# Routing stage of a fused attention and mixture-of-experts kernel: the two experts searched in the logits, softmax, token products and last remainders moved to GpSimd, other filler counts on TensorE

## What is computed

```
x = x + tanh(g_xattn[0]) * xattn(layernorm(x), ctx, itok, Wq, Wkv, Wo)
h_in = layernorm(x)
gate_logits = einsum('bsh,eh->bse', h_in, gate_w)          # E = 8
gate_probs = softmax(gate_logits, axis=-1)
top_v, top_i = top_k(gate_probs, 2)
comb_w = einsum('bsk,bske->bse', top_v, one_hot(top_i, E))
for e in range(E):
    h = silu(h_in @ w1[e] + b1[e])
    y = h @ w2[e] + b2[e]
    out = out + y * comb_w[..., e:e + 1]
x = x + tanh(g_ffn[0]) * out
```

## Time and profile before

| | |
|---|---|
| median of 3 runs | 357.06 us (356.36 to 357.26) |
| the profiled execution | 356.92 us, of which 355.1 us is the span from first to last instruction |
| TensorE, busy share of the span | 91% |
| VectorE | 76% |
| GpSimd | 58% |
| ScalarE | 49% |
| mean granted clock of TensorE | 0.978 of full |

### The profile page before, as it was taken

One profiled execution on the slowest core, in us unless ns is written; L12 is line 12 of the kernel. 1 busy time (PEld: TensorE's weight loads), 2 busy tenths in 40 slices (PEclk: granted clock), 3 DMA queues, 4 the chain that ended last, 5 costly groups with the idle time before them and its releaser, 6 DMA issues.

```text
span 355.1 us, 11441 instructions
## 1 busy us (share of the span) xinstructions
PE 322.9 (91%) x3486; PEld 266.3 (75%) x3486; DVE 269.9 (76%) x638; ACT 174.1 (49%) x490; POOL 205.9 (58%) x223
## 2 busy tenths in 40 slices
PE   8789989999977989999999999999999999999930
PEld 7457778888877877888888888888888887778710
DVE  5649999999978887778877788777887875656520
ACT  2452255565455456656555565654656543253400
POOL 3476889996752071566656757477473764662330
PEclk9999999999999899999999999999999999999985
DMA  7799999998999421232323323232332323241210
GB/s 250 246 362 412 405 420 404 404 351 327 344 384 391 119 64 34 32 60 37 56 38 64 46 47 48 50 61 38 57 48 48 53 42 61 35 68 26 33 18 13
DMA packets 31406, 53.23 MB, mean 150 GB/s; under 512 B 4834, under 2 KB 25554, under 8 KB 29300
## 3 DMA queue, kind: packets, MB, share of 16 engines
q0 software_dynamic: 9408, 26.63, 29.5%
q1 hardware_dynamic: 15972, 22.44, 17.6%
q10 hardware_dynamic: 5968, 3.39, 3.1%
HBM read 42.29 MB, written 10.17 MB: 148 GB/s over the span
## 4 chain that ended last, share of the span: by engine, by line
PE 63%; DVE 20%; issue 5%; DMA 5%; ACT 2%; POOL 2%; DVEq 0%; ACTq 0%; POOLq 0%
PE ps L1090 28%; PE ps L1104 16%; PE ps L1107 8%; DVE ps L1270 5%; DVE sel L1266 2%; PE ps L1118 2%; PE ps L1112 2%; DMA sel<-near_rows,win_near 2%; DVE w_parts L1266 2%; DMA tokens_split<-xsplit 2%; DVE xs L1302 1%; PE ps L1111 1%; PE ps L1106 1%; DMA near_rows<-w_parts 1%; DVE ps L1274 1%
## 5 line engine op out<-in xcount | busy, mean ns | idle before, releaser
L1090 PE MATMUL ps<-sel,w_parts 128*128 128x128 f16 x1776 | 141.3, 219 | 1.0 <-issue 1.0
L1090 PEld LDWEIGHTS ps<-sel,w_parts 128*128 x1776 | 119.3, 98 | 26.0 <-issue 1.8
L823 ACT ACTIVATE sel<-ps,b1T 128x128 f32<-128x128 f32 x296 | 84.3, 368 | 91.4 <-PE ps L1090 89.4
L596 POOL DMA_INDIRECT out<-sel x37 | 63.1, 1706 | 85.9 <-DVE sel L1540 74.0
L1104 PE MATMUL ps<-w_parts,sel 128*128 x259 | 96.3, 379 | 0.4
L1107 PE MATMUL ps<-w_parts,sel 128*128 x259 | 70.6, 273 | 0.0
L588 POOL DMA_INDIRECT sel<-tokens_split,sel x37 | 43.7, 1180 | 18.9 <-DVE sel L1463 12.6
L1495 DVE SCALAR_TENSOR_TENSOR sel<-sel 128x512 f16<-128x512 f32 x74 | 51.3, 694 | 2.5
L1481 DVE SCALAR_TENSOR_TENSOR w_parts<-w_parts (+1 forms) x32 | 39.0, 1220 | 8.4 <-issue 7.2
L1493 DVE TENSOR_SCALAR sel<-sel 128x512 f16<-128x512 f32 x74 | 33.2, 448 | 10.4 <-ACT sel L823 10.0
L583 POOL TENSOR_TENSOR sel<-sel 128x1 f32<-128x1 f32 x37 | 39.8, 1076 | 1.9 <-PE ps L1118 1.9
(11 more groups left out here) (221 smaller groups left out, 462.1 us busy)
## 6 DMA issues: line engine op xcount, KB each, us to landing
w_parts<-in_L_ffn_w SPq DMA_DIRECT2D x16, 1024.0 KB
out<-xs SPq DMA_DIRECT2D x16, 128.0 KB
tokens_split<-xsplit ACTq DMA_DIRECT2D x16, 128.0 KB, 6.2
xs<-in_x ACTq DMA_DIRECT2D x2, 512.0 KB, 7.1
xs<-in_x SPq DMA_DIRECT2D x2, 512.0 KB, 7.7
near_rows<-w_parts SPq DMA_DIRECT2D x4, 256.0 KB, 9.2
sel<-tokens_split,sel POOLq DMA_INDIRECT x37
out<-sel POOLq DMA_INDIRECT x37
```

Source lines behind the costliest of these rows:

```text
L596: pool.indirect_dma_start(out_rows, bass.IndirectOffsetOnAxis(slot_row[:, at(q - 1)], 0), y_sb[(k + 3) % 4], None, compute_op=ALU.add).the ...
L823: act.activation(h32[n][:, c * P:c * P + P], ps_h[n][:, c * P:c * P + P], ACT.Silu, bias=biases[:, c:c + 1], scale=1.0 / (X_SCALE * W_SCALE))\
L1090: mm = pe.matmul(ps_h[n][:, c * P:c * P + P], w, xx, start=(i == 0), stop=(i == len(products) - 1))
```

## The change

1. VectorE searches the two largest in the logits, not in the probabilities (`top_two`, then `chosen`), for tiles 0 to 10 and then 11 to 15. The subtraction of the largest logit is one GpSimd instruction over all 16 tiles, after the last of these searches; one Exp on ScalarE follows it. Sum and reciprocal stand on VectorE behind the scan, and three GpSimd products make `r_comb`.
2. The last two remainders stand on GpSimd behind these products.
3. The two products of `col_tok` with the token numbers go from VectorE to GpSimd; TensorE's first and third `rows_into_list` wait for them as well.
4. The fillers of the drain are 10, 10, 12 and 8 (before 4, 4, 8 and 4), and those ahead of `RT_CUM` 36 (before 48).

```diff
@@ GpSimd
             norms(T - 1, 1)
+            pool.wait_ge(s["rt"], RT_TOP)
+            pool.tensor_tensor(r_tmp[:, :, :], logit[:, :, :], r_m8[:, :, 0:1].to_broadcast([P, T, E]), ALU.subtract)\
+                .then_inc(s["shifts_ok"], 1)
+            pool.wait_ge(s["rt_exp"], 1)
+            pool.wait_ge(s["rt"], RT_CUM)
+            pool.tensor_scalar(r_p[:, :, :], r_ex[:, :, :], gate2[:, 0:1], None, ALU.mult).then_inc(s["comb_ok"], 1)
+            pool.wait_ge(s["comb_ok"], 1)
+            pool.tensor_tensor(r_p[:, :, :], r_p[:, :, :], r_m16[:, :, :], ALU.mult).then_inc(s["comb_ok"], 1)
+            pool.wait_ge(s["rt"], RT_INVERSE)
+            pool.wait_ge(s["comb_ok"], 2)
+            pool.tensor_tensor(r_comb[:, :, :], r_p[:, :, :],
+                               r_rs[:, :].rearrange("p (t o) -> p t o", o=1).to_broadcast([P, T, E]), ALU.mult)\
+                .then_inc(s["comb_ok"], 2)
             remainder(T - 2)
             remainder(T - 1)
-
+            for h in range(2):
+                tokens = slice(T // 2 * h, T // 2 * h + T // 2)
+                pool.wait_ge(s["rt"], RT_HOT + 1 + h)
+                pool.tensor_tensor(col_tok[:, tokens, :, :], col_tok[:, tokens, :, :], spread_pairs(tok16[:, :], NT),
+                                   ALU.mult).then_inc(s["tok_ok"], 1)
             pool.wait_ge(s["o_ps"], T)
             pool.memset(b2_wide, 0.0).then_inc(s["b2_zeroed"], 1)
@@ ScalarE
             token_out(T - 4)
-            act.wait_ge(s["rt"], RT_SHIFT)
-            act.activation(r_ex[:, 0:LATE, :], r_tmp[:, 0:LATE, :], ACT.Exp).then_inc(s["rt_exp"], 1)
             logits_kept(T - 4)
...
-            act.wait_ge(s["rt"], RT_SHIFT_LATE)
-            act.activation(r_ex[:, LATE:T, :], r_tmp[:, LATE:T, :], ACT.Exp).then_inc(s["rt_exp"], 1)
+            act.wait_ge(s["shifts_ok"], 1)
+            act.activation(r_ex[:, :, :], r_tmp[:, :, :], ACT.Exp).then_inc(s["rt_exp"], 1)
...
-            act.wait_ge(s["rt"], RT_COMB)
+            act.wait_ge(s["comb_ok"], 4)
             act.dma_start(xd.rearrange("(t p) d -> p t d", p=P)[:, :, D:XD], r_comb[:, :, :]).then_inc(s["comb_in"], 16)
@@ TensorE
             second_turn(T - 3)
-            spin(4)
+            spin(10)
             logits(T - 3)
             second_turn(T - 2)
-            spin(4)
+            spin(10)
             logits(T - 2)
+            spin(12)
+            second_turn(T - 1)
             spin(8)
-            second_turn(T - 1)
-            spin(4)
             logits(T - 1)
 
-            spin(48)
+            spin(36)
             pe.wait_ge(s["rt"], RT_CUM)
...
             pe.wait_ge(s["rt"], RT_ROWS)
+            pe.wait_ge(s["tok_ok"], 1)
             rows_into_list(0, 8)
...
             pe.wait_ge(s["rt"], RT_ROWS + 2)
+            pe.wait_ge(s["tok_ok"], 2)
             rows_into_list(16, 24)
@@ VectorE
+            def top_two(some):
                 dve.wait_ge(s["logit_ok"], some.stop)
...
-                    ins = v.max(r_m8[:, t, :], r_p[:, t, :])
+                    ins = v.max(r_m8[:, t, :], logit[:, t, :])
                 link(ins)
                 for t in range(some.start, some.stop):
-                    ins = v.max_index(r_i8[:, t, :], r_m8[:, t, :], r_p[:, t, :])
+                    ins = v.max_index(r_i8[:, t, :], r_m8[:, t, :], logit[:, t, :])
                 link(ins)
...
+            early, late = slice(0, T - 5), slice(T - 5, T)
+            top_two(early)
             residual(T - 1)
             second_moments(T - 1)
-            choose(slice(0, LATE), 0)
-            shifted_logits(slice(LATE, T))
-            assert done[0] == RT_SHIFT_LATE
-            choose(slice(LATE, T), 1)
+            chosen(early)
+            top_two(late)
+            assert done[0] == RT_TOP
+            chosen(late)
...
-            link(v.scalar_tensor_tensor(out=r_comb[:, :, :], in0=r_p[:, :, :], scalar=gate2[:, 0:1], in1=r_m16[:, :, :],
-                                        op0=ALU.mult, op1=ALU.mult))
-            assert done[0] == RT_COMB
+            dve.wait_ge(s["rt_exp"], 1)
+            link(v.tensor_reduce(r_sum[:, :], r_ex[:, :, :], AX_X, ALU.add))
+            link(v.reciprocal(r_rs[:, :], r_sum[:, :]))
+            assert done[0] == RT_INVERSE
...
-            for h in range(2):
-                dve.wait_ge(s["rt"], RT_HOT + 1 + h)
-                count(v.tensor_tensor(col_tok[:, halves_of[h], :, :], col_tok[:, halves_of[h], :, :],
-                                      spread_pairs(tok16[:, :], NT), ALU.mult))
```

More of the change, by code:

```diff
@@ L279, in flamingo_layer @@
             w_hi_ok w_lo_ok out_in
-            rt rt_exp rt_ps b2_zeroed row_ps row_ok pad_hot_ok pad_ps pad_ok span_ps span_ok from_ps from_ok prev_ok tables list_ps tile_ps tile_ok prev_ps comb_in
+            rt shifts_ok rt_exp comb_ok rt_ps tok_ok b2_zeroed row_ps row_ok pad_hot_ok pad_ps pad_ok span_ps span_ok from_ps from_ok prev_ok tables list_ps tile_ps tile_ok prev_ps comb_in
             slot_w_ok gathered0 gathered1 gathered2 gathered3 xT_ps xT_ok h_ps silu_ok hhi_ok hlo_ok y_half y_ps y_low_ok y_ok scattered out_done""".split()
@@ L331, in spread_mid, with spread_pairs @@
             return ap.rearrange("p (o c) -> p o c", o=1).to_broadcast([P, n, ap.shape[1]])
+        def spread_pairs(ap, n):
+            return ap.rearrange("p (n o i) -> p n o i", o=1, i=2).to_broadcast([P, ap.shape[1] // 2, n, 2])
         def place(v):
@@ L1336, in _, with chosen @@
             experts = iota[:, 0:E]
-            def shifted_logits(some):
+            def top_two(some):
                 dve.wait_ge(s["logit_ok"], some.stop)
[L1341 to L1350, removed]
                 for t in range(some.start, some.stop):
-                    ins = v.max(r_m8[:, t, :], r_p[:, t, :])
+                    ins = v.max(r_m8[:, t, :], logit[:, t, :])
                 link(ins)
                 for t in range(some.start, some.stop):
-                    ins = v.max_index(r_i8[:, t, :], r_m8[:, t, :], r_p[:, t, :])
+                    ins = v.max_index(r_i8[:, t, :], r_m8[:, t, :], logit[:, t, :])
                 link(ins)
+            def chosen(some):
+                n = some.stop - some.start
                 link(v.tensor_copy(r_i2[:, some, :], r_i8[:, some, 0:2]))
@@ L1362, in choose @@
                 link(v.tensor_tensor(r_m16[:, some, :], r_oh[:, 0, some, :], r_oh[:, 1, some, :], ALU.add))
-            shifted_logits(slice(0, LATE))
-            assert done[0] == RT_SHIFT
+            early, late = slice(0, T - 5), slice(T - 5, T)
+            top_two(early)
             residual(T - 1)
             second_moments(T - 1)
-            choose(slice(0, LATE), 0)
-            shifted_logits(slice(LATE, T))
-            assert done[0] == RT_SHIFT_LATE
-            choose(slice(LATE, T), 1)
+            chosen(early)
+            top_two(late)
+            assert done[0] == RT_TOP
+            chosen(late)
             link(v.tensor_tensor_scan(r_cum[:, :, :].rearrange("p e t -> p (e t)"), r_go[:, :, :].rearrange("p e t -> p (e t)"),
@@ L1413, in count @@
                 ins.then_inc(s["rt"], 1)
-            def spread_pairs(ap, n):
-                return ap.rearrange("p (n o i) -> p n o i", o=1, i=2).to_broadcast([P, ap.shape[1] // 2, n, 2])
             def over_pairs(n, width):
@@ L1543, in _ @@
             expert_steps(moe, 2, 1)
-RT_SHIFT, RT_SHIFT_LATE, RT_CUM, RT_COMB, RT_FIRST, RT_HOT, RT_ROWS, RT_ORDER = 2, 12, 21, 22, 29, 34, 39, 45
-RT_SLOT, RT_LIST, RT_PREV, RT_PLACES = 49, 52, 56, 57
+RT_TOP, RT_CUM, RT_INVERSE, RT_FIRST, RT_HOT, RT_ROWS, RT_ORDER, RT_SLOT, RT_LIST, RT_PREV, RT_PLACES = \
+    7, 11, 13, 20, 25, 28, 34, 38, 41, 45, 46
 TURN_AT = 2
```

## The result

| | before | changed |
|---|---|---|
| median | 357.06 us | 359.24 us (358.64 to 360.87, 5 runs) |
| ratio of changed to before | | 1.0076 (95% interval 1.0046 to 1.0107) |
| the profiled execution | 356.92 us, span 355.1 | 360.62 us, span 358.9 |
| TensorE's mean granted clock | 0.978 | 0.968 |
| last logits kept, from | 108.51 | 110.09 |

The last line says that the whole difference arises ahead of that step. The profiled execution of the changed kernel took 1.4 us more than its median, so its +3.7 us is more than the median's +2.2.

A forecast was written before the change was run, and what follows sets the result against it. VectorE's first step on the list (122.21) was taken to decide. Later pad work (+1.4 us) and low clock (+1.7) put it at 125.15, +2.9 us: 356.92 + 2.9 = 359.8, range 356.0 to 361.6.

The forecast's parts named there:

- the case that it called the likeliest: TensorE making the list at the lower clock level: 359.8 us, own range 358.9 to 361.2, chance 0.48.
- The scan: VectorE behind the last logits: the scan ends 1.37 us earlier, about 111.5.
- ScalarE behind the remainders: Table load waits for the last remainder (114.6); 6.25 us later TensorE's product of `pad_hot` starts, 120.85 not 119.44: +1.4 us.
- The clock: TensorE idles some 5 us, then makes the list at half speed at first: 4.25 us for 2.58, +1.7.
- GpSimd against VectorE: Token products and `row_hot` exclude each other; factors and list by 122.2 to 123.6, the 0.79 us saved lost again.
- VectorE's wait at the list: Sign of being right: VectorE waits 3 us or more ahead of its first step on the list.
- The drain: End of attention: earlier copies (-0.2) and more fillers (+0.24) cancel; last logits at 108.7 as now.
- The sum: VectorE's first step on the list at 125.15 against 122.21: +2.9 us, 359.8 in all.
- A: Rival: clock stays at 2.4 GHz or is back in time for the list; +1.3 us, 358.2, chance 0.15.
- D: Rival: GpSimd's token products on f16 pairs cost twice as much, 2.5 us each; +4.0 us, 360.9, chance 0.07.
- B: Rival: no GpSimd collisions, or table load ahead of the waiting `token_out`; 0 to +0.8 us, 357.3, chance 0.14.
- C: Rival: pad work doesn't hold the list, VectorE's chain stays the bound; -1.37 - 0.79, up to 354.8, chance 0.16.

The follow-up runs named there:

- experiment 1: Changed kernel with the last two remainders ahead of GpSimd's subtraction again; 356.95 us, ratio to before 1.0011.
- experiment 4: Changed kernel with 84 fillers in place of 8 ahead of TensorE's wait for `pad_hot`; 357.55 us, ratio to before 1.0022.
- experiment 3: Changed kernel with the two token products back on VectorE; 358.91 us, ratio to before 1.0050.
- experiment 10: Changed kernel with remainders ahead of GpSimd's subtraction and 36 fillers for 8 ahead of the wait for `pad_hot`; 357.05 us, ratio to before 1.0003.
- experiment 6: Kernel before with the changed filler counts alone (10, 10, 12, 8 and 36); 356.89 us, ratio to before 1.0000.
- experiment 9: Changed kernel with remainders ahead of GpSimd's subtraction and token products on VectorE; 356.20 us, ratio to before 0.9968.
- 8: Changed kernel with remainders ahead, token products on VectorE and 36 fillers for 8 ahead of the wait for `pad_hot`; 355.26 us, ratio to before 0.9959.

## Why the prediction came out right

The forecast was 359.8, the median is 359.24; the case that it called the likeliest is the one that happened. Point by point:

- **The scan.** Predicted 1.37 us earlier behind the last logits; 3.90 us (108.51 to 112.41) became 2.61 (110.09 to 112.70), 1.29 less. Right.
- **ScalarE behind the remainders**, the term that decides. The remainders were to end 3.1 us behind the scan (111.5 to 114.6); 3.25 (113.12 to 116.37). The table load is released by them, as predicted, and experiment 1 shows it by taking it away. From there to the product of `pad_hot` 6.25 us were predicted and 5.66 measured (116.37 to 122.03), too large by 0.6: I had the issue of the transfer of `r_comb` between the table load and the Abs, and it went out 0.06 us after the load began, beneath it.
- **The clock.** Idle some 5 us, measured 4.65; list in 4.25 us, measured 4.00; against 2.58 at the high level. So +1.4 for +1.7, and experiment 4 shows that it is the clock. But that the size came out near is partly luck, because two errors cancel. I had the low level last 3.3 us from the product's start, as in the trace of before, and double the time of all that fell in it. It lasted from between 120 and 121 to between 127 and 128, past the end of the list; and the list at the low level took 1.55 times as long, not twice: 1.77 us (122.03 to 123.80) for 1.00 (119.44 to 120.44) from the product to the first group, but 2.23 for 1.58 from there to its end, where a group took 0.47 for 0.36. The Trainium skill (TensorE: Matmul & The Clock Gate, Part 1) has the array's clock halved when it has been idle and whole again under load; the trace agrees, 1.00 in 118 to 120, 0.82 in 120 to 121 and 0.50 in 123 to 124.
- **GpSimd against VectorE.** A pair of pieces of `row_hot` took 3.35 us in place of 1.29, and the step L1405 took 0.69 in place of 0.22, ending at 115.82 just after the first remainder's half of 1.30 us from 115.07. I had put the end of factors and list at 122.2 to 123.6, no bound against 125.15; it was hidden, as experiment 3 shows, and it is about 1.5 us when nothing hides it (experiment 10). The Trainium skill (SBUF — State Buffer, Who interferes with whom) has a VectorE instruction with two SBUF inputs and a GpSimd one that reads SBUF exclude each other for a whole instruction: the first piece ran from 118.68 to 120.40 across the first product (to 119.85), the second to 122.03 across the second product (to 121.48). The trace agrees.
- **VectorE's wait at the list.** I had named 3 us or more as a sign of being right; it was 1.63. Three would have needed VectorE done at the early end of my range. Between the last of `row_hot` and the list stand three more steps, down to L1456, which my sum left out (121.46 to 122.18 before; now to 124.55), and the list ended 0.6 us earlier behind the last logits than I had it. This sign failed without touching the time.
- **The drain.** Predicted unchanged; right for the fillers (experiment 6) and wrong for the profiled execution, where the last logits came 1.58 us later, 1.25 of it between the rounding of tile 13 and the last logits (5.34 us became 6.59; experiment 1, with the same fillers at the high level, has 5.43). The same fall is in 6 of the 12 profiled executions, one of each kernel, experiment 6 with nothing but other filler counts among them, and it is why the profiled one stands at +3.7.
- **The sum.** +2.9 predicted. Counted from the last logits, which leaves the drain out, VectorE's step came at 16.08 us (110.09 to 126.17) for 13.70, +2.4. The prediction's 16.64 (108.51 to 125.15) less 0.59 behind the remainders and 0.20 in the list (I had used 4.2), plus 0.19 up to the remainders' end and 0.04 behind the list, is that 16.08; the medians differ by 2.2.
- The **rivals** A (clock stays up) and D (dearer products) did not happen; experiment 4 is A made by hand, 357.55 where A said 358.2, and 0.6 of that is the term that was too large behind the remainders. B's early table load did not happen either: the load was released by the last remainder. Nor did C, which needed the product of `pad_hot` by 117.5; it came at 122.03.

What each part costs, by the ratios: parts 1 and 4 together -0.3% (experiment 9); part 3 on top +0.4% (1); part 2 on top +0.8% (3); both +1.1%. That this is less than their sum is within the noise of the times; that one hides beneath the other is what the profiles show (13.46 and 13.47 us from the scan in experiment 3 and the changed kernel, 9.93 and 11.41 in 8 and 10). Part 1 was worth having, and parts 2 and 3 together cost some three times what it gave.

Left open: why the clock falls in the drain in some executions and not in others, why it fell in the list of experiment 1 (2.07 us without a matmul ahead of it) and not in that of 9 (2.08 us), and what 36 fillers in place of 8 ahead of the product of `pad_hot` are worth. The wait of `first_half` for a transfer (0.88 us before, 1.35 in the changed kernel), behind which TensorE sits idle 1.5 us, wasn't tried.

## What to carry to other kernels

Before an instruction is moved back on a helper engine, follow its consumer's queue and not only its result: here two remainders of 1.3 us were moved 6 us, and with them a table load, eight Abs and a Relu that have nothing to do with them. An elementwise operation moved from VectorE to GpSimd need not be off VectorE's path: here VectorE's instructions beside it read two operands from SBUF, and two of them took 3.35 us for 1.29. Price such a pair as if both ran on one engine. And when a chain gets shorter, fillers that fitted it can become a hold-up: count them again, at the low clock too (48 took 5.28 us for 2.84).

## What the runs showed of the hardware that was not expected

A DMA issue on ScalarE's queue did not wait for a table load ahead of it (load 116.76 to 118.04, issue at 116.82), though both had waited for a token transfer ahead of them. Two instructions of VectorE and two of GpSimd that exclude each other took turns, one of each, though each engine had its next one queued: the pieces of `row_hot` ended at 120.40 and 122.03, the products at 119.85 and 121.48. In the expert stage of the kernel before, a GpSimd product was held across two VectorE instructions in a row. The clock fell to 1.2 GHz at the end of the drain in 6 of 12 profiled executions; in the changed kernel's it took 6.59 us from the rounding of tile 13 to the last logits (103.50 to 110.09), against 5.43 in experiment 1, with the same fillers at the high level (101.42 to 106.85).
